# Centred output weights, one VectorE instruction for each residual, and outputs that leave five tiles behind: a transformer block with a routed feed-forward part on one Trainium2 core

## The reference

```
x = x + layernorm(attention(layernorm(x)))
x = x + layernorm(ffn(layernorm(x)))

attention: q, k, v = projections of the normed x, q and k through elu + 1
           running sums over the sequence of k*v (per head, 8 x 8) and of k
           values = (q . sum kv) / (q . sum k + 1e-6);  result = values @ Wo + bo
ffn:       logits = x @ w_router.T; each token has one expert of 16 (top 1)
           shared = silu(x @ w_gate.T) * (x @ w_up.T) @ w_down.T
           expert = silu(gate) * up of score*x, @ down_proj[expert]
           result = shared + expert
layernorm: (x - mean) / sqrt(var + 1e-5), no gain, no offset
```

## Time and profile before

| | us |
|---|---|
| median of 3 runs | 351.54 (349.24 to 351.72) |
| the profiled execution, its own time | 347.56 |
| its span, first to last instruction | 345.8 |
| busy in the span: PE / DVE / ACT / POOL | 264.6 / 286.4 / 186.6 / 192.7 |
| TensorE clock granted, mean | 0.913 of 2.4 GHz |

### The profile page before, as it was taken

One profiled execution on the slowest core, in us unless ns is written; L12 is line 12 of the kernel. 1 busy time (PEld: TensorE's weight loads), 2 busy tenths in 40 slices (PEclk: granted clock), 3 DMA queues, 4 the chain that ended last, 5 costly groups with the idle time before them and its releaser, 6 DMA issues.

```text
span 345.8 us, 6250 instructions
## 1 busy us (share of the span) xinstructions
PE 264.6 (77%) x1465; PEld 184.2 (53%) x1465; DVE 286.4 (83%) x1138; ACT 186.6 (54%) x572; POOL 192.7 (56%) x221
## 2 busy tenths in 40 slices
PE   3459999999998995638887988821999999999000
PEld 1125556555554553325555655521999889988000
DVE  5998999999999999996998787640379999999930
ACT  2524656565665552257666664203899888885000
POOL 5056777767775863200054556570007888888870
PEclk9988999999999998967999899985899999999655
DMA  6999900000000000000011111126950101110000
GB/s 187 374 426 396 396 4 0 2 3 0 2 0 2 2 0 0 1 1 2 1 62 64 63 62 64 64 100 229 355 166 18 35 31 43 41 36 29 25 2 0
DMA packets 13668, 28.39 MB, mean 82 GB/s; under 512 B 1950, under 2 KB 10150, under 8 KB 12610
## 3 DMA queue, kind: packets, MB, share of 16 engines
q1 hardware_dynamic: 10448, 21.57, 17.1%
q0 software_dynamic: 3040, 6.37, 5.4%
q10 hardware_dynamic: 146, 0.07, 0.1%
HBM read 15.38 MB, written 13.60 MB: 84 GB/s over the span
## 4 chain that ended last, share of the span: by engine, by line
PE 39%; DVE 24%; POOL 18%; issue 12%; DMA 4%; ACT 1%; POOLq 0%; ACTq 0%; SPq 0%; another core or an unknown queue 0%; DVEq 0%
PE banks L1009 13%; POOL out L490 10%; POOL rows L484 6%; PE banks L1028 5%; PE banks L1100 5%; DVE hT L814 2%; PE banks L1037 2%; PE banks L1134 2%; POOL sorted_rows L474 2%; DVE stats L641 2%; DMA rows<-in_x 2%; PE banks L997 2%; DVE num L740 1%; DVE rows L857 1%; DVE stats L849 1%
## 5 line engine op out<-in xcount | busy, mean ns | idle before, releaser
L1009 PE MATMUL banks<-kv,upto 128*128 128x512 f32 x128 | 63.5, 621 | 1.3 <-POOL kv L449 1.3
L449 POOL TENSOR_TENSOR kv<-qk,vv 128x1024 f32<-128x1024 f32 x32 | 62.4, 1950 | 2.5
L1134 PE MATMUL banks<-xsT,w_now 128*128 128x128 f32 x376 | 52.6, 284 | 0.4 <-DVE hT_e L948 0.4
L490 POOL DMA_INDIRECT out<-rows,token_i x47 | 46.8, 997 | 9.8 <-issue 8.2
L443 POOL TENSOR_TENSOR qk<-ex,rl 128x256 f32<-128x256 f32 x32 | 23.3, 727 | 47.0 <-ACT ex L546 47.0
L1134 PEld LDWEIGHTS banks<-xsT,w_now 128*128 128x128 f32 x376 | 47.1, 197 | 1.2 <-issue 0.7
L474 POOL DMA_INDIRECT sorted_rows<-rows,slot_i x32 | 31.7, 992 | 28.7 <-DVE slot_i L804 20.7
L718 DVE TENSOR_TENSOR prod<-banks,qk 128x1024 f32<-128x1024 f32 x32 | 38.9, 1216 | 2.1 <-PE banks L1009 1.5
L740 DVE TENSOR_REDUCE num<-prod 128x128 f32<-128x1024 f32 x32 | 38.7, 1208 | 0.3 <-DVE den L735 0.3
L948 DVE TENSOR_TENSOR hT_e<-silu_e,banks 128x256 f32<-128x256 f32 x47 | 19.4, 412 | 19.8 <-ACT silu_e L623 16.1
L484 POOL TENSOR_TENSOR rows<-rows,yn 128x128 f32<-128x128 f32 x40 | 19.1, 477 | 28.0 <-DVE yn L940 26.1
(11 more groups left out here) (158 smaller groups left out, 640.0 us busy)
## 6 DMA issues: line engine op xcount, KB each, us to landing
sorted_rows<-rows SPq DMA_DIRECT2D x3, 1950.0 KB, 13.3
rows<-sorted_rows SPq DMA_DIRECT2D x11, 520.0 KB, 6.3
w_exp<-in_gate_up SPq DMA_DIRECT2D x4, 1024.0 KB, 19.7
w_exp_down<-in_down SPq DMA_DIRECT2D x4, 512.0 KB, 19.7
rows<-in_x SPq DMA_DIRECT2D x1, 1024.0 KB, 11.1
rows<-in_x SPq DMA_DIRECT2D x1, 768.0 KB, 8.4
out<-rows,token_i POOLq DMA_INDIRECT x47
sorted_rows<-rows,slot_i POOLq DMA_INDIRECT x32
```

Of the source, the lines that this page charges most:

```text
L449: nc.gpsimd.tensor_tensor(kv[:, u, :].rearrange("p (h m d) -> p h m d", h=NH, m=HD), k, v, ALU.mult).then_inc(s_kv, 1)
L490: nc.gpsimd.indirect_dma_start(out=out_rows, out_offset=bass.IndirectOffsetOnAxis(ap=token_i[:, j - 1:j], axis=0), in_=rows[:, j - 1, 0:D] ...
L1009: ins = nc.tensor.matmul(ps_s[u % 2][:, cols], upto[:], kv[:, u, cols], start=True, stop=True)
L1134: ins = nc.tensor.matmul(ps_gue[u % 2][:, c * P:(c + 1) * P], w_now[:, u % 2, c * P:(c + 1) * P], xsT[:, u % 2, :], start=True, stop=True)
```

## The change

Three things are changed.

1. Wo, bo, w_down and all 16 down_proj are centred on the chip: the mean over the output features is taken off each row (`centre_steps`: a reduction and a `scalar_tensor_tensor` with the sum broadcast). Then the results of attention and ffn have mean zero, and the two norms need a scale only. DVE centres bo and Wo ahead of the first statistics, w_down in step 4 of stage 1 (one instruction after `zq`, one after `carry`), and down_proj in four pieces of 1024 columns between the routing and stage 3. PE waits for each where it first uses them, ACT's first `bias_row` for the first two.
2. In stage 2 `ya` is gone, on ACT and as a tensor. DVE adds each tile with one `scalar_tensor_tensor`, x + scale * result. `rstd_steps` there stays as it is.
3. In stage 3 `yn` and POOL's add are gone. The norm has 11 steps (`scale_steps`) for 14. DVE writes x + scale * result in one `scalar_tensor_tensor` (`outputs`), five steps after the tile's own for eight. POOL only waits and issues the scatter.

```
+def scale_steps(nc, series, st, width, scratch, rs):
+    mean_even, sq_even, sq_odd = st[1], st[2], st[5]
+    ve, y, t = scratch[0:3]
+    tensor, scalar, fused = nc.vector.tensor_tensor, nc.vector.tensor_scalar, nc.vector.scalar_tensor_tensor
+    series.wait()
+    yield series.done(tensor(t, mean_even, mean_even, ALU.mult))
+    yield series.done(fused(out=ve, in0=sq_even, scalar=width * EPS, in1=sq_odd, op0=ALU.add, op1=ALU.add))
+    series.wait()
+    yield series.done(fused(out=ve, in0=ve, scalar=1.0 / width, in1=t, op0=ALU.mult, op1=ALU.add))
+    series.wait()
+    yield series.done(scalar(y.bitcast(I32), ve.bitcast(I32), -0.5, RSQRT_MAGIC, ALU.mult, ALU.add))
+    series.wait()
+    yield series.done(tensor(t, y, y, ALU.mult))
+    series.wait()
+    yield series.done(tensor(t, t, ve, ALU.mult))
+    series.wait()
+    yield series.done(fused(out=t, in0=t, scalar=-10.0 / 3.0, in1=t, op0=ALU.add, op1=ALU.mult))
+    series.wait()
+    yield series.done(fused(out=y, in0=t, scalar=5.0, in1=y, op0=ALU.add, op1=ALU.mult))
+    series.wait()
+    yield series.done(tensor(t, y, y, ALU.mult))
+    series.wait()
+    yield series.done(fused(out=t, in0=t, scalar=-27.0 / 1024.0, in1=ve, op0=ALU.mult, op1=ALU.mult))
+    series.wait()
+    yield series.done(fused(out=rs, in0=t, scalar=0.5625, in1=y, op0=ALU.add, op1=ALU.mult))
+SCALE_STEPS = 11
+def centre_steps(nc, series, rows_of, sums, ready=None):
+    n, width = rows_of.shape[1], rows_of.shape[2]
+    yield series.done(nc.vector.tensor_reduce(sums, rows_of, AX, ALU.add))
+    series.wait()
+    ins = nc.vector.scalar_tensor_tensor(
+        out=rows_of, in0=sums.rearrange("p (n o) -> p n o", o=1).to_broadcast([P, n, width]), scalar=-1.0 / width,
+        in1=rows_of, op0=ALU.mult, op1=ALU.add)
+    yield ins.then_inc(ready, 1) if ready else ins
...
-            for j in range(ST + 1):
-                if j < ADDED_BY_POOL:
-                    r = flat(rows[:, j:j + 1, 0:D])
-                    pool.wait_ge(s_yn, j + 1)
-                    nc.gpsimd.tensor_tensor(r, r, yn[:, j % 4, :], ALU.add).then_inc(s_fin, 1)
-                if j > 0:
-                    if j <= ADDED_BY_POOL:
-                        pool.wait_ge(s_fin, j)
-                    else:
-                        pool.wait_ge(s_fin_last, j - ADDED_BY_POOL)
-                    nc.gpsimd.indirect_dma_start(
-                        out=out_rows, out_offset=bass.IndirectOffsetOnAxis(ap=token_i[:, j - 1:j], axis=0),
-                        in_=rows[:, j - 1, 0:D], in_offset=None,
-                        bounds_check=NTOK - 1, oob_is_err=False).then_inc(s_out, 16)
+            for j in range(ST):
+                pool.wait_ge(s_fin, j + 1)
+                nc.gpsimd.indirect_dma_start(
+                    out=out_rows, out_offset=bass.IndirectOffsetOnAxis(ap=token_i[:, j:j + 1], axis=0),
+                    in_=rows[:, j, 0:D], in_offset=None,
+                    bounds_check=NTOK - 1, oob_is_err=False).then_inc(s_out, 16)
...
-            act.wait_ge(s_bias, 16)
+            act.wait_ge(s_centred_o, 2)
...
-                if live(s + 3, NG):
-                    act.wait_ge(s_norm2, s + 4)
-                    for k in range(GT):
-                        c = tiles(GT * (s + 3) + k)
-                        ins = nc.scalar.activation(
-                            ya[:, (u + 1) % 2, k * D:(k + 1) * D], flat(rows[:, c, D:2 * D]),
-                            ACT.Identity, bias=nmean2[:, 1, c], scale=rstd2[:, 1, c])
-                        if k % 2:
-                            ins.then_inc(s_ya, 1)
...
+            centring = Series(dve, s_centre, 0)
+            dve.wait_ge(s_bias, 16)
+            finish(centre_steps(nc, centring, bias[:].rearrange("p (n d) -> p n d", n=1), row_sums[:, 0:1])
+                   ).then_inc(s_centred_o, 1)
+            dve.wait_ge(s_w, 16)
+            finish(centre_steps(nc, centring, w_o.rearrange("p (n d) -> p n d", n=1), row_sums[:, 1:2])
+                   ).then_inc(s_centred_o, 1)
             dve.wait_ge(s_x[0], 16)
             setup.done(finish(stats_of(*CHUNKS[0])))
...
-                    for half in range(2):
-                        dve.wait_ge(s_ya, 2 * (s + 2) + 1 + half)
-                        xg = rows[:, tiles(GT * (s + 2) + 2 * half, 2), 0:D]
-                        yield nc.vector.tensor_tensor(
-                            xg, xg, ya[:, u % 2, 2 * half * D:2 * (half + 1) * D].rearrange("p (t d) -> p t d", d=D),
-                            ALU.add).then_inc(s_x1, 1)
-                    dve.wait_ge(s_x1, 2 * (s + 3))
+                    dve.wait_ge(s_norm2, s + 3)
+                    for k in range(GT):
+                        t = GT * (s + 2) + k
+                        x1 = flat(rows[:, tiles(t), 0:D])
+                        yield nc.vector.scalar_tensor_tensor(
+                            out=x1, in0=flat(rows[:, tiles(t), D:2 * D]), scalar=rstd2[:, 1, tiles(t)], in1=x1,
+                            op0=ALU.mult, op1=ALU.add).then_inc(s_x1, 1)
+                    dve.wait_ge(s_x1, GT * (s + 3))
...
-            run_steps(dve, step1, 0, 4, 28, 28, 8, 4)
+            run_steps(dve, step1, 0, 4, 28, 4, 8, 4)
+            dve.wait_ge(s_w2, 16)
+            shared = centre_steps(nc, centring, w_d, row_sums[:, 0:FC], s_centred_d)
+            step1(4, 0, shared, 1)
+            run_steps(dve, step1, 5, 4, 28, 28, 8, 4)
...
+            dve.wait_ge(s_wexp, 16 * (E // 4) * 2)
+            for e in range(0, E, 4):
+                ins = finish(centre_steps(nc, centring, w_exp_down[:, e:e + 4, :, :].rearrange("p e c d -> p (e c) d"),
+                                          row_sums[:, e * FC:(e + 4) * FC]))
+            ins.then_inc(s_centred_e, 1)
+            def norm_quad(q, n, norm):
+                c = tiles(4 * q, n)
+                dve.wait_ge(s_stats3, min(4 * (q + 1), ST))
+                yield nc.vector.tensor_scalar(token_i[:, c], rows[:, c, TOKEN], -1.0, float(NTOK), ALU.mult, ALU.add)
+                for ins in scale_steps(nc, norm, [stats3[:, 0:n, k] for k in range(6)], D,
+                                       [scratch3[:, k, 0:n] for k in range(3)], rstd3[:, q % 2, 0:n]):
+                    yield ins
+            def outputs(q, first, last):
+                dve.wait_ge(s_series3, SQ * (q + 1))
+                for i in range(4 * q + first, min(4 * q + last, ST)):
+                    x1 = flat(rows[:, tiles(i), 0:D])
+                    nc.vector.scalar_tensor_tensor(out=x1, in0=flat(rows[:, tiles(i), D:2 * D]),
+                                                   scalar=rstd3[:, q % 2, i % 4:i % 4 + 1], in1=x1,
+                                                   op0=ALU.mult, op1=ALU.add).then_inc(s_fin, 1)
...
-                if live(j - 8, ST):
-                    i = tiles(j - 8)
-                    if u == 0:
-                        dve.wait_ge(s_series3, SQ * (q - 1))
-                    if live(j - 12, ST):
-                        dve.wait_ge(s_fin, min(j - 11, ADDED_BY_POOL) if isinstance(j, int) else j - 11)
-                    nc.vector.tensor_scalar(yn[:, u, :], flat(rows[:, i, D:2 * D]), rstd3[:, parity, u:u + 1],
-                                            nmean3[:, parity, u:u + 1], ALU.mult, ALU.add).then_inc(s_yn, 1)
-                if u:
-                    norm_step()
-                at_least(dve, s_sum, min(j, ST) if isinstance(j, int) else j)
+                        next(norms3, None)
+                if j > 0:
+                    dve.wait_ge(s_sum, min(j, ST))
...
                 if live(j - 1, ST):
                     nc.vector.bn_stats(stats3[:, (u + 3) % 4, :],
                                        flat(rows[:, tiles(j - 1), D:2 * D])).then_inc(s_stats3, 1)
-                norm_step()
-                if live(j - 8, ST) and isinstance(j, int) and j - 8 >= ADDED_BY_POOL:
-                    dve.wait_ge(s_yn, j - 7)
-                    nc.vector.tensor_tensor(flat(rows[:, i, 0:D]), flat(rows[:, i, 0:D]), yn[:, u, :],
-                                            ALU.add).then_inc(s_fin_last, 1)
+                if u:
+                    norm_step()
                 if live(j, ST):
                     r = flat(rows[:, tiles(j), D:2 * D])
                     dve.wait_ge(s_de, j + 1)
                     nc.vector.tensor_tensor(r, ps_ye[u % 2][:, 0:D], r, ALU.add).then_inc(s_sum, 1)
-                norm_step(NORM_STEPS[u])
-                if u == 3:
-                    norm_step(20)
...
-            run_quads(dve, step3, -1, 3, 11, QUADS + 2)
+            for j in range(-4, 4 * QUADS):
+                q, u = j // 4, j % 4
+                step3(q, u)
+                if u == 0 and live(q - 1, QUADS):
+                    norms3 = norm_quad(q - 1, min(4, ST - 4 * (q - 1)), Series(dve, s_series3, SQ * (q - 1)))
+                for _ in range((5, 5, 0, 0)[u]):
+                    next(norms3, None)
+                if u == 0 and live(q - 2, QUADS):
```

(9 more changed lines are left out.)

42 lines of the change are left out of this document (11 added, 31 removed).

## The result

| | kernel before | changed kernel | ratio |
|---|---|---|---|
| first measurement, median | 350.46 us (349.24 to 351.72, 4 runs) | 364.23 us (361.34 to 365.60, 4 runs) | 1.038, interval 1.030 to 1.046 |
| the same program, measured again beside other kernels | 345.83 us (17 runs) | 337.62 us (335.21 to 337.98, 4 runs) | 0.975, interval 0.969 to 0.980 |

The change made the kernel slower by 3.8% where the prediction said 3% faster. Measured again, the same program was 2.5% faster. Both kinds of result came back. I call the conditions of the first kind strained and those of the second calm: in three of the eight measurements the kernel before took 350.5 to 351.8 us, in the other five 345.3 to 346.7. One chip number stands beside a measurement of either kind, so the chip alone is not shown to be the cause.

A forecast was written before the change was run, and what follows sets the result against it. POOL was taken to hold stage 3's pace, PE and ACT after the change. Terms 0.85 + 1.2 + 0.6 + 0.5 - 9.6 - 4.4 = -10.85 took the median 351.54 to 340.7 us, range 337 to 346.5.

The forecast's parts named there:

- Stage 3, pace: Stage 3: without its add POOL no longer sets the pace, PE and ACT do at 1.46 us a tile; -9.6 us.
- the norm's hump in step 1: Stage 3: step 1 alone needs about 2.1 us of DVE, hidden while PE has its `hT_e`; 0.3 us once.
- The end: End of stage 3: last scatter starts 7.7 us after the last sum, against 12.07; -4.4 us.
- The start: Start of the kernel: DVE waits for bo and centres it and Wo ahead of the first statistics; +0.85 us.
- w_down in step 4: Stage 1, step 4: centring w_down comes ahead of `prod` and its second instruction meets POOL's `kv`; +1.2 us.
- Stage 2 and down_proj: Stage 2's adds become four of 128 columns, +0.6 us; down_proj's centring may hold POOL's scatters on the chain, +0.5.
- The cover of down_proj: Before stage 3: 9.6 us of DVE centring hidden where DVE was idle, ending near 239.4 with 4 us to spare.
- (a): Stage 3: DVE becomes the bound at about 1.55 us a tile, or the step-1 hump reaches PE; 344.6 us, chance 0.20.
- (b): Before stage 3: centring of down_proj holds POOL's scatters on the chain, at the upper bound of 2.2 us; 342.4, chance 0.10.
- (c): Stage 3: something unseen besides POOL holds the pace, so only the end gains; 350.3 us, chance 0.05.
- (d): Stage 3: each output instruction waits for the scatter of the tile before, 1.92 us a tile; 360.1 us, chance 0.05.

The follow-up runs named there:

- spread kernel: Changed kernel with each quad's norm spread over its four steps and one output in each: 338.56 us, ratio 0.978, calm; 356.13 us, ratio 1.015, strained.
- doubled landings: Changed kernel plus a second, plain store of every finished tile from SP's queue, beside POOL's scatter: 337.41 us, ratio 0.975, calm.

## Why the prediction was wrong

**Stage 3, pace: the step that failed.** It said that POOL's scatter, "1.29 us from one to the next where nothing else holds it, under the 1.45 of PE and ACT", no longer sets the pace, and that "PE and ACT bound the stage again". POOL didn't set the pace by its own work in either condition; that part was right. What the sum left out is what the scatters' new timing does to others. In the strained conditions of the first measurement PE's semaphore increments are held for up to 3.3 us behind POOL's four scatters in 3.9 us, and ACT, DVE and PE stand still for them: +14.5 us for -9.6. In the profile of before no output scatter starts less than 1.65 us after the one ahead of it until the last sum, since the adds lie between them. The text listed scatters "never back to back at 1.29 before the last sum" as what would show the step right, and they were back to back, in both conditions, from the first quad on: DVE hands three outputs out 0.99 us apart, after the norm's hump in step 1. I had seen the hump, and priced it for PE alone (0.3 us once).

In calm conditions the same step was off by its size only: 43 tiles in 64.50 us, 1.500 each, for 63.1. 1.4 us are the hump, since the spread kernel has 63.15. The output instruction was taken to be as short as an add and isn't:

```profile
L971 DVE SCALAR_TENSOR_TENSOR rows<-rows,rstd x47: 337/344/352, 263.3 to 350.3; 128x128 f32<-128x128 f32 x47
```

This is in nanoseconds, for the 279 to 292 of the earlier trace rows. It reads its scale from a tensor; line 163, of the same form with a constant for a scale, took 0.29 us above. By the earlier trace rows PE stands still for 7.67 of 65 us before; it is 2.42 of 59 in the calm profile.

**The end**: -3.7 for -4.4. The last scatter starts 8.40 us after the last sum for the forecast 7.7, in both conditions: six steps of 1.29 behind the one that starts 0.67 after the sum. The forecast had the output of that tile 0.4 ahead of it.

**The start**: +1.02 for +0.85 (8.56 for 7.54). The four instructions take 1.05 from 7.51, for 1.06; bo landed 0.2 later than I reckoned with. In the profiles of the changed kernel these statistics start at 7.70 to 8.62, so when bo lands moves this term by as much as its size.

**w_down in step 4**: right where it stands. `prod` of this step starts 2.32 us after `kv` does, for 1.11 before (40.60 and 39.49), in each of ten profiles with the centring that I compared: +1.21 for +1.2. The row above shows why, 1.08 us beside `kv`. The Trainium skill's rule cited there, page "SBUF — State Buffer", agrees: the instruction ends at 43.66, 0.28 after `kv` does (41.43 and 1.95), as if it had waited for all of it. The recorded 1.4 was a little high by its own terms: 41.44 and 0.33 are 41.8, not 42.0.

How much of this stays on the chain is another matter. From tile 25 on `att` runs 2.25 us later than before (119.49 for 117.24), of which 1.02 are the start; the rest, 1.23, looks like the forecast by luck. Reckoned from the first statistics, `att` of tile 25 comes after 110.93 us in both pairs, for 109.70 and 109.72 before, but after 109.97 to 110.01 in three more profiles of the changed kernel. The difference of 0.9 is there ahead of step 4: the granted clock from 24 to 26 us is 0.70 and 0.71 in the two, and 0.98 to 1.00 in the three. Without it only 0.3 of the 1.2 is left at tile 25, so the chain had slack where the text saw "little slack that could take it up".

**Stage 2 and down_proj**: +0.16 for +1.1 in the calm pair, where the first down product of the shared part is 3.26 us later (165.88 to 169.14), and the sum of tile 3 3.42; in the strained pair it is +1.46 (5.69 and 7.15). The cover of down_proj held: in the calm profile DVE ends the four pieces at 242.18, 4.40 us ahead of its first `hT_e`. What was not in the sum is the boundary of stages 1 and 2: from the +2.5 of tile 25's `att` in the calm pair (119.55 for 117.07) to +3.26, and 3.4 in the strained pair (2.25 to 5.69). In the profiles of both pairs the granted clock is 0.50 to 0.56 from 150 to 160 us; from 160 to 170 it is 1.00 and 0.74 before, 0.59 in the changed kernel. Among executions of the changed kernel and its spread version the first down product lies between 163.78 and 169.14, so this term is not fixed by the code alone.

**The rivals.** (a)'s 1.55 a tile did not come, but one way that it named did, in calm conditions: the hump of step 1 reached PE, for 1.4 us. (b) fell, as stage 2 and down_proj together cost 0.16 in the calm pair. (c) fell, as the pace changed in both conditions. (d) named the right family, that more scatters in the way of others make it slower, but as an output instruction that waits for a scatter; its instruction took 337 to 352 ns in the strained profile and the calm one, and that its 360.1 is near 364.2 is an accident. The strained result is a fifth case that had no chance in the text.

The range of 337 to 346.5 took in 337.6 and 337.7 of the calm measurements, with 336.9 just under it. That is in part luck, since the sum started from a strained time of the kernel before: from the calm 345.8 it would have given 335.0. The calm difference is -8.2 for -10.85.

**What stays open.** Shown: in strained conditions PE's increments arrive late behind scatters, records are missing, and both kernels lose stage-2 time; the spread outputs halve the loss of stage 3; neither a chip number, nor bursts, nor doubled landings bring it about by themselves. Not shown is what makes conditions strained. It isn't in the program, since the same one ran in both; whether it was something else on the chip, nothing here tells. Only argued: that what is strained is the path on which semaphore changes are recorded. For it speaks that records are missing, three quarters of them landings of scatters, and that the five increments come out like a queue being emptied. The Trainium skill, page "NOTIFIC — the notification-queue block", section "Overflow: three behaviours, one of which stalls the engine", says that this block's inner pipeline holds its producers back rather than lose a record. The traces agree with holding back, if PE is the one held. They also lack records, which that section has only where a queue's ring is full; no run here shows whether one was. Every execution timed here was recorded, so whether the stalls exist without a recording is not known. Nor is it shown that scatters 1.69 us apart would avoid them in the changed kernel; the strained stage 3 of the kernel before, at 1.65 and more, speaks for it.

## What to carry to other kernels

When an edit takes work from between two transfers, ask what else the faster rhythm meets, and not only which engine is next: here four scatters 1.29 us apart, for some 1.7 before, turned a gain of 8 us in stage 3 into a loss of 14 under some conditions. Run the changed kernel again beside every experiment: three experiments without a stall seemed to prove a theory, until the unchanged program ran without one as well. When a wait is put down to nothing that can be named, look at when the awaited semaphore was recorded against when its instruction ended.

## What the runs showed of the hardware

- PE's increments can be held for 3.3 us and come out 34 to 93 ns apart, while those of DVE, ACT and POOL are in time; a trace can lack 22% of the semaphore records.
- A VectorE instruction of 128 columns that reads its scale from a tensor took 345 ns, the same form with a constant 0.29 us.
- The same program took 364.2 and 337.6 us, 8% apart, each within 1.3% over its four runs; the kernel before moved by 1.5% between the same conditions, 350.5 and 345.4.
- A register load of ACT from SBUF takes 0.56 us one after the other, and nothing where ACT's work covers it (337.7 us with the loads, 337.4 without).
- From the start of the last scatter to the end of the program 9.03 to 9.07 us pass in every profile that has scatters. With plain stores from SP's queue the program ends 11 us earlier behind its last `silu_e` (10.7 for 21.6), POOL's seven scatters behind the last sum included.
